# The weighted values of a unit in two halves, with scores and a tile of row maxima between

## The chip, the core and the metric

The kernel runs on one core of a Trainium2 chip. Its engines are TensorE (matmuls; in the profile PE, its weight loads PEld), VectorE (DVE), ScalarE (ACT), GpSimd (POOL) and SyncE (SP, which issues most DMAs). They run side by side, each in its own program order, and wait for each other by semaphores. The metric is the device time of one execution in microseconds.

## The reference

Input are 64 sequences x of 128 tokens with 128 features, a side input of the same shape, and a context of 64 x 120 x 128. Layer one is

```
x = x + L0_xattn(layernorm(x), side, ctx, ctx)   # 16 heads of 8, 128 + 120 keys
x = x + L0_ffn(layernorm(x))                     # top 2 of 8 experts, 352 wide
```

and layer two has the same form: attention over the 120 context keys, then a gelu layer with the top 2 of 8 experts. In the attention of layer one, queries come from the normalised x, the first 128 keys and values from the side input by projection, the other 120 keys and values are the context itself. Scores are q.k / sqrt(8), softmax over all 248 keys, weighted values, an output projection with bias, and the residual.

## The kernel before

The 64 sequences are handled in 16 groups of four. Layer one's attention runs first, with the routing of its expert layer beside it; then come the expert matmuls (135 tiles of 128 routed rows), then layer two's attention and its expert layer. The change touches layer one's attention alone.

One step of the loop handles one group g and has 8 units: unit u is one sequence (u // 2) and one half of its 16 heads (u % 2). What a unit issues, and in which order, is a list written by hand, UNIT (line 144). Every engine walks through the same list and takes what concerns it:

- "scores" i, four a unit (line 979, matmuls in line 993): transposed scores of four heads, keys in the partitions, for group g. Places 0 and 2 have the 128 side keys, 1 and 3 the 120 context keys. Four matmuls of 128 columns, into one of three PSUM tiles (ps_sc). The row maxima are already in the contraction as rows of their own. ScalarE takes each tile through the exponent into p (line 674).
- "max" i, four a unit (matmuls in line 1006): scores of the *next* group g+1, two heads a tile, queries in the partitions, 2 matmuls of 248 columns into one of two PSUM tiles (ps_mx). VectorE reduces each to its negated row maxima (row_maxima, line 822). Behind the reduction stand small pieces of statistics and routing (between, INPUT_STAGES, ROUTE_STAGES).
- "values" 0 and 1 (weighted_values, matmuls in line 1030): the weighted values of the unit *before*, of one half of its eight heads each. 18 columns of weights (8 value columns and one of ones for each of two heads), four strips of 32 output partitions, float32: 8 matmuls a half, which the trace records as 16. Half 0 waits for the exponents of places 0 and 1 of the unit before, half 1 for those of 2 and 3, and signals pv_done when it is through. The same PSUM tile ps_o collects four units; after units 0 and 4 ScalarE evicts it to o_sb (line 703) once pv_done has reached the unit, and behind its exponents of that unit.
- "job" 0, 1 and 2: what the list jobs (line 127) puts at this place of this unit: transposes (XT, line 939; AT of the attention's output, line 963; OB of the values, line 959; MT of the maxima, line 955; RX), projections (QP, KP, VP, OP), router matmuls (RQ line 1349, RC). They share two PSUM tiles (misc) in turn, so a job waits until the one before the last has been evicted.

TensorE takes all four kinds, ScalarE "scores" and "job", VectorE "max" and "job". pv_done is also what ScalarE waits for before it writes the first exponent of a unit into p's tile of two units before.

Of the kernel before, what the change touches and what calls it, by code (L numbers as in the profile page):

```python
# [101 lines left out]
def attention_layer(nc, x_in, x_out, side_t_in, ctx_in, ctx_t_in, layer, consts, route, stacks, second, expert_w=None,  # L102
# [40 lines left out]
    if first:  # L143
        UNIT = [
            ("job", 0), ("scores", 0), ("max", 0), ("scores", 1), ("job", 1), ("max", 1), ("values", 0),
            ("values", 1), ("scores", 2), ("max", 2), ("scores", 3), ("job", 2), ("max", 3),]
    else:
        UNIT = [
            ("job", 0), ("scores", 0), ("max", 0), ("scores", 1), ("values", 0), ("values", 1), ("job", 1),
            ("max", 1),]  # L150
# [1855 lines left out]
def encoder(nc, a, out):  # L2006

    x3 = nc.dram_tensor("x3", (NG, S, GB, D), F32, kind="Internal").ap()
    xs = nc.dram_tensor("routed_in", (ROUTED_ROWS, ROW), F32, kind="Internal").ap()
    ys = nc.dram_tensor("routed_out", (TOKENS * TOP + 2 * E * S, D), F32, kind="Internal").ap()  # L2010
    x1, second = (ys[0:TOKENS * TOP].rearrange("(g k s b) d -> k g s b d", k=TOP, s=S, b=GB)[k] for k in range(TOP))
    with ExitStack() as c:
        route, stacks = Route(nc, c, xs), Stacks(nc, c)
        consts = constants(nc, c, a["w_attn"], a["b_attn"], a["b_rows"], a["wqkv_t"], route)
        attention_layer(nc, a["x"], x1, a["side_t"], a["ctx"], a["ctx_t"], 0, consts[0], route, stacks, second,
                        expert_w=(a["w1_t"], a["w2_t"]))
        expert_tiles(nc, ys, route, stacks)
        head = AdapterHead(nc, c, route, x3, a["wg_t"], a["bg"], a["W1_t"], a["W2_t"])
        attention_layer(nc, x1, x3, None, None, a["ctx_t"], 1, consts[1], route, stacks, second, head=head)
        adapter_layer(nc, x3, out, head)  # L2020
# [46 lines left out]
```

## Time and profile before

| | |
|---|---|
| median of 3 runs | 1438.31 us (1438.08 to 1440.24) |
| profiled execution | 1436.72 us |
| its span, first to last instruction | 1434.9 us |
| mean granted TensorE clock | 0.956 of full speed |
| weighted values in layer one | first block 73.9 us, last 577 us into the span |

The span is what the trace covers; the profiled execution's own time has 1.8 us around it. The page's busy times are by engine over the whole span. For the change one reads the stretch of layer one: how long a group takes there, and at which times TensorE starts each block of matmuls. Starts are measured; ends of matmuls are modelled, so a block's cost is read from its start to the start of the next.

### The profile page before, as it was taken

The page shows a single profiled execution, that of the slowest core. Times are in us where ns is not written, and L with a number is a line of the kernel's source. Part 1 is how long each engine was busy: PE and PEld are TensorE (multiplying, and loading weights), DVE is VectorE, ACT ScalarE, POOL GpSimd, SP SyncE. Part 2 cuts the span into 40 slices and gives each one's busy share as a digit, 9 for nine tenths or more (in the row PEclk, how much of TensorE's full clock was granted, in tenths as well). Part 3 has the DMA queues.
Part 4 walks back from the last instruction along what each step waited for, and adds up shares of the span by engine and source line. Part 5 has one row for each costly group of instructions (what it writes and reads, how often), then busy time and mean ns, then how long its engine had stood idle before and what let it go on. Part 6 is the DMA issues. An engine that isn't in the chain of part 4 may idle for free. (4 is left out here: it accounts for less than half of the span.)

```text
span 1434.9 us, 44416 instructions
## 1 busy us (share of the span) xinstructions
PE 1271.0 (89%) x16309; PEld 1052.2 (73%) x16309; DVE 1083.2 (75%) x3396; ACT 828.7 (58%) x1582; POOL 875.1 (61%) x947
## 2 busy tenths in 40 slices
PE   1789999999999999279999999669999999869997
PEld 0367787777777787279999999437777778746775
DVE  6778999989988896547766666458888888736663
ACT  1167777767777767156666666235666666534452
POOL 5346888888888856547777777544555544136650
PEclk9799999999999999689999999879999999979999
DMA  5676677777777760535555554588888887445765
GB/s 167 220 220 212 216 248 245 235 225 251 240 233 225 219 193 30 194 53 64 65 65 65 64 65 63 103 235 224 265 271 268 260 264 234 127 104 120 178 166 131
DMA packets 212422, 252.15 MB, mean 176 GB/s; under 512 B 38256, under 2 KB 173680, under 8 KB 205040
## 3 DMA queue, kind: packets, MB, share of 16 engines
q1 hardware_dynamic: 179552, 226.33, 52.7%
q0 software_dynamic: 25840, 21.71, 10.8%
q8 instruction: 131, 2.15, 0.6%
q10 hardware_dynamic: 6816, 1.29, 0.5%
q14 instruction: 83, 0.68, 0.1%
HBM read 156.73 MB, written 91.46 MB: 173 GB/s over the span
## 5 line engine op out<-in xcount | busy, mean ns | idle before, releaser
L822 DVE TENSOR_REDUCE L_neg_max<-L_ps_mx 128x2 f32<-128x496 f32 (+1 forms) x768 | 489.1, 660 | 93.4 <-PE L_ps_mx L1006 90.7
L674 ACT ACTIVATE L_p<-L_ps_sc 120x512 f32<-120x512 f32 (+1 forms) x768 | 417.3, 598 | 207.5 <-PE L_ps_sc L993 203.9
L1006 PE MATMUL L_ps_mx<-stack_k,stack_q 118*128 118x248 bf16 (+1 forms) x2048 | 299.7, 251 | 45.8 <-DMA stack_q<-L_q_rows 29.9
L993 PE MATMUL L_ps_sc<-stack_q,stack_k 122*120 122x128 bf16 (+1 forms) x3072 | 300.3, 222 | 5.0 <-DMA stack_q<-L_mT 2.4
L993 PEld LDWEIGHTS L_ps_sc<-stack_q,stack_k 122*120 122x120 bf16 (+1 forms) x3072 | 239.3, 123 | 58.2 <-issue 34.4
L1507 POOL DMA_INDIRECT routed_out<-M_y,M_x x135 | 211.9, 1570 | 88.5 <-DVE M_y L1598 87.3
L1030 PE MATMUL L_ps_o<-L_p,L_v 120*18 120x128 f32 (+1 forms) x6144 | 219.7, 275 | 3.3 <-ACT L_o_sb L703 2.9
L1006 PEld LDWEIGHTS L_ps_mx<-stack_k,stack_q 118*128 118x128 bf16 x2048 | 141.9, 100 | 106.7 <-issue 36.5
L1030 PEld LDWEIGHTS L_ps_o<-L_p,L_v 120*18 120x18 f32 (+1 forms) x6144 | 147.3, 98 | 38.1 <-issue 24.8
L1377 POOL DMA_INDIRECT routed_in<-R_xn,R_slot x128 | 127.1, 993 | 42.5 <-issue 35.9
L1553 ACT COPY M_w<-stack_k 128x768 f32 x135 | 112.1, 832 | 53.9 <-PE M_ps_g L1530 36.9
L1530 PE MATMUL M_ps_a<-M_xT,M_w 128*128 128x128 f32 x810 | 114.0, 278 | 0.0
L1530 PE MATMUL M_ps_g<-M_xT,M_w 128*128 128x128 f32 x810 | 113.4, 277 | 0.0
L1539 PE MATMUL M_ps_y<-M_w,M_hT 128*128 128x128 f32 x810 | 112.7, 276 | 0.0
L488 POOL TENSOR_TENSOR L_rem<-L_qf,L_q_parts_sb 128x512 f32<-128x512 f32 x30 | 34.8, 1161 | 121.4 <-ACT L_q_parts_sb L619 121.4
L1558 ACT ACTIVATE M_act_a<-M_ps_a 128x384 f32<-128x384 f32 x135 | 66.2, 491 | 73.4 <-PE M_ps_a L1530 72.4
L1530 PEld LDWEIGHTS M_ps_a<-M_xT,M_w 128*128 128x128 f32 x810 | 102.4, 194 | 0.1
L1530 PEld LDWEIGHTS M_ps_g<-M_xT,M_w 128*128 128x128 f32 x810 | 102.3, 194 | 0.0
L1539 PEld LDWEIGHTS M_ps_y<-M_w,M_hT 128*128 128x128 f32 x810 | 101.3, 192 | 0.2 <-DVE M_hT L1590 0.2
L1579 DVE COPY M_w<-stack_q 128x384 f32 x135 | 49.1, 363 | 63.7 <-issue 61.5
L1590 DVE TENSOR_TENSOR M_hT<-M_act_a,M_ps_g 128x384 f32<-128x384 f32 x135 | 74.8, 554 | 27.5 <-ACT M_act_a L1558 22.8
L1967 DVE TENSOR_TENSOR F_hg<-F_h,F_spread 128x512 f32<-128x512 f32 x64 | 41.3, 689 | 48.5 <-DMA F_spread<-F_gate_rows 39.5
(210 smaller groups left out, 2127.3 us busy)
## 6 DMA issues: line engine op xcount, KB each, us to landing
L_q_rows<-L_q_parts_sb SPq DMA_DIRECT2D x192, 192.0 KB, 4.1
stack_q<-L_q_rows SPq DMA_DIRECT2D x192, 192.0 KB
stack_k<-L_k_rows SPq DMA_DIRECT2D x96, 372.0 KB
stack_k<-L_k_rows SPq DMA_DIRECT2D x96, 180.0 KB
F_spread<-F_gate_rows SPq DMA_DIRECT2D x32, 512.0 KB, 6.5
L_k_rows<-L_k_parts_sb SPq DMA_DIRECT2D x32, 372.0 KB, 4.2
M_x<-routed_in SPq DMA_DIRECT2D x135, 66.0 KB, 2.0
L_k_rows<-L_k_parts_sb SPq DMA_DIRECT2D x32, 180.0 KB, 4.2
```

What stands on the lines that cost most here:

```text
L674: nc.scalar.activation(p_t[t][u % 2][:, quarter * 4 * S:(quarter + 1) * 4 * S], ps_sc[n % NSC][0:KEYS[t], :], ACT.Exp).then_inc(sc_read, 1)
L822: nc.vector.tensor_reduce(neg_max[:, b, kk * HPB:(kk + 1) * HPB], v, AX.X, ALU.max, negate=True).then_inc(max_read, 1)
L993: last = mm(ps_sc[n % NSC][0:KEYS[t], j * S:(j + 1) * S], k_st[p][:, b // 2, h, b % 2, k0:k0 + KEYS[t]], q_st[p][:, b // 2, h, b % 2], sta ...
L1006: last = mm(ps_mx[i % NMX][:, j * NK:(j + 1) * NK], q_st[p][0:TERM_TOP, b // 2, h, b % 2], k_st[p][0:TERM_TOP, b // 2, h, b % 2], start=Tr ...
L1030: last = mm(ps_o[r:r + 2 * (DH + 1), col:col + S], v_t[t][p][:, b, at:at + 2 * (DH + 1)], p_t[t][u % 2][:, j * S:(j + 1) * S], start=(t == ...
L1377: self.nc.gpsimd.indirect_dma_start(out=self.route.xs, out_offset=bass.IndirectOffsetOnAxis(ap=self.slot[g.par][:, b, k:k + 1], axis=0), i ...
L1507: nc.gpsimd.indirect_dma_start(out=ys, out_offset=bass.IndirectOffsetOnAxis(ap=token_row, axis=0), in_=y_t[ts % NY][:], in_offset=None, co ...
L1530: last = nc.tensor.matmul(out[:, k * S:(k + 1) * S], w1[th % NW][:, half + k * 128:half + (k + 1) * 128], xT[p][:], start=True, stop=True)
L1539: last = nc.tensor.matmul(ps_y[p][:, 0:D], hT[p][:, k * S:(k + 1) * S], w2[ty % NW][:, k * D:(k + 1) * D], start=(k == 0), stop=(k == FC - 1))
L1553: nc.scalar.copy(w1[tw % NW][:], w1_all[:, bass.ds(e_w * W1, W1)]).then_inc(w1_ready, 1)
L1558: nc.scalar.activation(act_a[p][:], ps_a[p][:, 0:FC * S], ACT.Silu).then_inc(silu_ready, 1)
L1590: nc.vector.tensor_tensor(hT[p][:], act_a[p][:], ps_g[p][:, 0:FC * S], ALU.mult).then_inc(hT_ready, 1)
```

## The change

In layer one's UNIT the entry ("values", 1) moves from directly behind ("values", 0) to behind ("max", 2), ahead of ("scores", 3). By count of places the tiles of row maxima are max 0 to 3, so it stands between the third and the fourth. Nothing else is edited, and layer two's list is unchanged.

```
     if first:
         UNIT = [
             ("job", 0), ("scores", 0), ("max", 0), ("scores", 1), ("job", 1), ("max", 1), ("values", 0),
-            ("values", 1), ("scores", 2), ("max", 2), ("scores", 3), ("job", 2), ("max", 3),]
+            ("scores", 2), ("max", 2), ("values", 1), ("scores", 3), ("job", 2), ("max", 3),]
```

## Rows read from the trace of the kernel before

**Rows 1.** The page, busy time by engine over the span.

```profile
PE 1271.0 (89%) x16309; PEld 1052.2 (73%) x16309; DVE 1083.2 (75%) x3396; ACT 828.7 (58%) x1582; POOL 875.1 (61%) x947
```

**Rows 2.** Windows of one group: length; busy PE, PEld, DVE, ACT, POOL; clock; DMA.

```profile
169.64:201.62 31.98, 31.32 (x514) 25.43 (x513) 29.56 (x98) 23.39 (x49) 27.54 (x31) 1.00 0.77 241
331.55:363.54 31.99, 31.32 (x514) 25.43 (x513) 29.57 (x98) 23.39 (x49) 27.55 (x31) 1.00 0.74 235
```

**Rows 3.** Waits in 331.55 to 363.54: us in total, times, longest.

```profile
DVE L_neg_max L822 <- PE L_ps_mx L1006: 1.9, 4, 0.9
```

**Rows 4.** Timeline of TensorE, 387.9 to 389.7: start, length, instructions.

```profile
387.92 0.38 PE L1006 MATMUL L_ps_mx<-stack_k,stack_q 118*128 118x248 bf16 x2
388.23 1.08 PE L1030 MATMUL L_ps_o<-L_p,L_v 128*18 128x128 f32 x32
389.24 0.40 PE L993 MATMUL L_ps_sc<-stack_q,stack_k 122*128 122x128 bf16 x4
389.47 0.38 PE L1006 MATMUL L_ps_mx<-stack_k,stack_q 118*128 118x248 bf16 x2
389.69 0.39 PE L993 MATMUL L_ps_sc<-stack_q,stack_k 122*120 122x128 bf16 x4
```

**Rows 5.** Timeline, unit 5: start and last four of one block of values.

```profile
348.96 0.53 PE L1030 MATMUL L_ps_o<-L_p,L_v 128*18 128x128 f32 x12
...
349.74 0.29 PE L1030 MATMUL L_ps_o<-L_p,L_v 120*18 120x128 f32 x4
349.97 0.40 PE L993 MATMUL L_ps_sc<-stack_q,stack_k 122*128 122x128 bf16 x4
```

**Rows 6.** Timeline, units 4 and 5: TensorE, and ScalarE's chain beside it.

```profile
346.50 0.39 PE L993 MATMUL L_ps_sc<-stack_q,stack_k 122*120 122x128 bf16 x4
346.98 0.39 PE L1006 MATMUL L_ps_mx<-stack_k,stack_q 118*128 118x248 bf16 x2
347.29 0.24 PE L955 MATMUL L_misc<-C_ident_bf,L_m_parts 128*64 128x128 bf16 x1
347.47 0.40 PE L993 MATMUL L_ps_sc<-stack_q,stack_k 122*128 122x128 bf16 x4
...
347.92 0.27 ACT L634 COPY L_mT<-L_misc 64x128 bf16<-64x128 bf16 x1
...
348.19 0.63 PE L959 MATMUL L_misc<-C_ident,L_o_sb 128*128 128x128 f32 x4
```

**Rows 7.** Timeline, start of unit 6: TensorE's scores and maxima, VectorE's reductions.

```profile
350.65 1.83 DVE L822 TENSOR_REDUCE L_neg_max<-L_ps_mx 128x2 f32<-128x496 f32 x3
...
350.86 0.39 PE L993 MATMUL L_ps_sc<-stack_q,stack_k 122*128 122x128 bf16 x4
351.37 0.39 PE L1006 MATMUL L_ps_mx<-stack_k,stack_q 118*128 118x248 bf16 x2
```

**Rows 8.** Timeline, end of unit 7 and start of unit 0.

```profile
357.49 0.38 PE L1006 MATMUL L_ps_mx<-stack_k,stack_q 118*128 118x248 bf16 x2
...
357.90 1.26 DVE L822 TENSOR_REDUCE L_neg_max<-L_ps_mx 128x2 f32<-128x496 f32 x2 [0.24 <-PE L_ps_mx L1006]
...
358.14 0.39 PE L993 MATMUL L_ps_sc<-stack_q,stack_k 122*128 122x128 bf16 x4
358.73 0.37 PE L1006 MATMUL L_ps_mx<-stack_k,stack_q 118*128 118x248 bf16 x2 [0.20 <-DVE L_neg_max L822]
...
359.22 0.39 PE L1006 MATMUL L_ps_mx<-stack_k,stack_q 118*128 118x248 bf16 x2
```

**Rows 9.** Timeline, units 0 and 2: VectorE's pair of reductions, and TensorE's job AT.

```profile
361.22 1.36 DVE L822 TENSOR_REDUCE L_neg_max<-L_ps_mx 128x2 f32<-128x496 f32 x2
...
366.75 0.39 PE L993 MATMUL L_ps_sc<-stack_q,stack_k 122*120 122x128 bf16 x4
367.39 0.63 PE L963 MATMUL L_misc<-C_ident,L_att 128*128 128x128 f32 x4 [0.25 <-DVE L_att L757]
```

**Rows 10.** Timeline, unit 1 of an earlier group: the key projection.

```profile
297.66 1.10 PE L946 MATMUL L_misc<-L_srcT,C_w 128*128 128x512 f32 x2 [1.51 <-DMA L_srcT<-in_side_t]
```

More of the change, by code:

```diff
@@ L145, in attention_layer @@
             ("job", 0), ("scores", 0), ("max", 0), ("scores", 1), ("job", 1), ("max", 1), ("values", 0),
-            ("values", 1), ("scores", 2), ("max", 2), ("scores", 3), ("job", 2), ("max", 3),]
+            ("scores", 2), ("max", 2), ("values", 1), ("scores", 3), ("job", 2), ("max", 3),]
     else:
```

## The prediction

> **What bounds the kernel now.** I read the page's busy shares, then the busy time of single groups of layer one, then the waits in one of them, then TensorE's order of time unit by unit. The page gives TensorE 89% of the span and no other engine over 75% [rows 1], but that is a mean over stages. In layer one the work repeats every 31.98 or 31.99 us, with 514 recorded matmuls each time: TensorE is busy 31.3 of the 32.0 us, VectorE 29.6, ScalarE 23.4, at a granted clock of 1.00, which is the 2.4 GHz level [rows 2]. The reader should doubt the 31.3, since matmul ends are modelled, and look at starts instead: inside a unit each block starts when the one before it has streamed: four scores take 0.22 to 0.23 us, a tile of maxima 0.22, and only a few waits stand between. VectorE itself waits four times for a tile, 1.9 us [rows 3]. So TensorE is the bound most of the time; VectorE takes over in stretches. The waits that I find between TensorE's starts, each what a step took over its usual 0.22 us, are 0.26 us in unit 4, 0.29 from unit 5 to 6, 0.36 and 0.05 from unit 7 to 0, and 0.41 ahead of the transposes of the attention in unit 2: about 1.4 us of 32 [rows 6 to 9].
>
> **The price of a switch.** The weighted values are matmuls with 18 columns of weights, written to four strips, and everything around them uses 120 or 128 columns. A tile of maxima is followed by scores after 0.22 us, but by values after 0.31: 0.09 to go in [rows 4]. Within a block of values four strips start every 0.11 us (28 matmuls in 349.74 - 348.96 = 0.78). The last four are followed by scores after 0.23 instead of 0.11: 0.12 to come out [rows 5]. The 64-column transpose of the maxima pays the same: 0.31 into it, and 0.18 out of it where a 128-column matmul at full rate leaves after 0.05 [rows 6]. There is no wait in this that another engine could end sooner: it stands in every unit, also where all inputs are old. I call it a switch: in and out cost 0.09 + 0.12 = 0.21 us.
>
> **The change, part by part.** Only TensorE's order changes, since VectorE and ScalarE skip the "values" entries and keep theirs; no DMA, no job and no matmul is added or removed. (1) The 32 matmul records of a unit's values were one block of 1.01 us; they become two of 16 with scores and a tile of maxima between. That is one switch more in each of 16 x 8 = 128 units: 0.21 x 128 = 26.9 us if nothing hides it. (2) The third scores and the third tile of maxima come 0.44 us earlier behind the first half: counted from the start of the first half, third scores at 0.56 (was 1.01), third maxima 0.80 (1.24), second half 1.10, fourth scores 1.67 (1.46), fourth maxima 1.90 (1.68). VectorE gets its third tile 0.44 us earlier and its fourth 0.22 later; ScalarE likewise. (3) The count that releases the probability tile comes 0.66 us or so later: with switch, half a block and the scores and maxima between. Queued behind it is only the first exponent of the next unit, whose scores come at least 0.8 us behind the second half, and the eviction of the values, which stands behind the fourth exponent anyway. I take nothing for it; if that cover failed, it would cost at most the 0.66 us in the two units a group that evict, 1.3 us a group, less than nothing I exclude, as no producer gets faster by it.
>
> **What of the 0.21 lies beside a wait.** I follow one group, lateness against the old times:
> - Units 2 to 3, 3 to 4 and 6 to 7 have no TensorE wait: +0.21 each, +0.64.
> - Unit 4: the fourth maxima waited 0.26 us for VectorE (346.50 to 346.98 instead of 0.22) [rows 6], so they start when they did, but the fourth scores are 0.21 later, and from them hangs ScalarE's chain of exponent, eviction of the values, copy of the maxima (347.92), whose bank the transposes of the values take at 348.19. The old exponent had started 0.05 behind its scores' readiness, so this chain is 0.16 later: +0.16.
> - Unit 5 to 6: 0.51 instead of 0.22 between scores and maxima, as VectorE runs three reductions without a gap [rows 7]. The lateness that TensorE brings is swallowed but for what VectorE's own chain has been set back: -0.07.
> - Unit 7 to 0: no job stands between. The first maxima of unit 0 waited for the reduction that began at 357.90 [rows 8]; that tile comes earlier now, and this 0.36 goes. What is late next is the second one: it needs the fourth maxima of unit 7 read, which lie ready 0.41 us behind the start of their matmuls (357.49 to 357.90), at 1.68 + 0.41 before and at 1.90 + 0.41 now; plus 0.68 for the reduction and 0.06 from its end to the next tile (357.90 + 1.26 to 359.22) [rows 8] it is 3.05 against 2.78 by TensorE. 3.05 + 0.31 = 3.36 to the next values, was 3.28: +0.07.
> - Units 0 to 2: the 0.41 before the transposes at 367.39 [rows 9] is VectorE's backlog. It would hide 0.43 almost whole, but the backlog itself moves: in unit 0 the pair of reductions takes 1.36 us instead of 1.25 [rows 9], so it already waits for the fourth tile, which is now 0.21 later. +0.22.
> Sum: 0.64 + 0.16 - 0.07 + 0.07 + 0.22 = 1.02 us a group, 0.7 of 1.7 hidden. Over 16 groups 16.3 us. Bounds from the same rows: all 1.4 us of waits hidden leaves 1.7 - 1.4 = 0.3 a group, 5 us; none hidden 26.9. The first group has more waits, and three groups wait for the side input (at 297.66 for 1.51 us in the row [rows 10]), which more time per group can only shorten: I take 1.0 off, an estimate with ends of 0 and 4. The sum is +15.3 us.
>
> The profiled execution took 1436.7 us, span 1434.9; it becomes 1452.0. The median of the runs is 1438.3, 1.6 above, and becomes **1453.6 us**. What comes behind layer one starts when its last group is done, so I shift it whole.
>
> **A rule to weigh.** By starts TensorE sets the pace, and by busy time VectorE has 29.6 of 32.0 us [rows 2]. The Trainium skill (Perfetto Trace Analysis, Identifying the Most-Contended Engine) says that TensorE's matmul busy share misleads and is to be judged by its weight loads' share; by that TensorE has 25.4 of 32.0, VectorE is the busiest, and the switches would be free. That is rival C below; I trust the starts over the shares.
>
> **Rivals.**
> - A, nothing hidden: +26.9 us, 1465. For it: three units of eight have no wait at all, and new waits could replace those removed. Against: the waits in units 4, 5 and 2 are set by VectorE, whose work is unchanged.
> - B, nearly all hidden: +5 us, 1443. For it: waits of 1.4 us a group and VectorE at 92%. Against: waits hide only what comes ahead of them in the same stretch, and VectorE has gaps of 0.2 to 0.9 us in units 6 to 7 that show TensorE as the bound there.
> - C, VectorE is the bound and the extra lies beside it: within 0.2%, 1438. Against: VectorE waits 1.9 us a group for tiles [rows 3].
> - D, the other side: faster. One mechanism: a 16-record block enters and leaves without the drain, since its neighbours are ready, and the earlier third tile takes away the waits at 358.73 and in unit 5. Without a price the third tile 0.44 earlier saves 0.14 us in unit 7 to 0 and up to 0.29 in unit 5 to 6: 0.43 a group, 7 us, 1431. It decides from a switch of under 0.7 / 8 = 0.09 us, the part that waits can hide. Against: the 64-column transpose, a block of a single matmul, pays full price in and out.
>
> **Chances.** Forecast 0.70 (+9 to +21 us), A 0.12, B 0.09, C 0.04, D 0.05. A measurement can tell about 0.2%, 3 us. The range 1443 to 1465 leaves out C, D and part of A. Faster 0.05, same 0.04, slower 0.91.
>
> **What would show it.** In the changed kernel: two values blocks of some 0.56 us from start to following scores, each entered 0.31 behind a tile of maxima or, for the second, likewise; a unit without waits 0.21 longer; steady groups of about 33.0 us; VectorE's waits for tiles grown to some 2.9 us a group; no wait at the first maxima of unit 0, one of 0.27 at the second; the wait before the attention's transposes down to 0.2 or less. Stages behind layer one keep their length. Wrong it would be if a half block left in under 0.5 us, or if the groups stayed at 32.0 us.

## The result, and the profile after

The changed kernel takes 1456.79 us in the median of four runs, the kernel before 1439.28 beside it: a ratio of 1.0124 with an interval of 1.0083 to 1.0164, slower, +17.5 us. Run again in five rounds, it gave 1454.26 us against the 1439.53 of before, +14.7 us, and a ratio of 1.0097 (1.0062 to 1.0132). The forecast was 1453.6, range 1443 to 1465. The profiled execution took 1463.31 us, span 1461.5, which is the slowest of the four; so it has to be read by stages before anything is concluded from it.

The windows of the four stages, before: layer one's attention, its routing end and experts, layer two's attention, the rest. Columns: stretch, its length, then busy PE, PEld, DVE, ACT, POOL with counts, granted clock, DMA share, GB/s.

```profile
73.90:577.40 503.50, 483.44 (x8009) 391.70 (x8008) 441.88 (x1407) 361.33 (x738) 386.74 (x437) 1.00 0.69 213
577.40:970.50 393.10, 330.99 (x2825) 316.29 (x2813) 251.02 (x756) 200.80 (x310) 253.54 (x179) 0.91 0.52 95
970.50:1267.40 296.90, 278.46 (x4523) 223.09 (x4522) 249.04 (x719) 186.07 (x366) 131.34 (x150) 0.99 0.77 230
1267.40:1434.90 167.50, 145.56 (x850) 106.82 (x838) 90.59 (x414) 67.05 (x146) 72.11 (x136) 0.93 0.61 148
```

The same stages of the changed kernel.

```profile
73.90:595.30 521.40, 513.65 (x8005) 373.55 (x8008) 449.14 (x1407) 371.49 (x739) 385.46 (x437) 1.00 0.66 205
595.30:991.20 395.90, 331.62 (x2825) 316.65 (x2815) 251.26 (x756) 200.95 (x310) 253.68 (x179) 0.90 0.53 95
991.20:1293.10 301.90, 281.26 (x4524) 225.01 (x4522) 248.49 (x719) 186.62 (x366) 131.33 (x150) 0.97 0.76 226
1293.10:1461.50 168.40, 147.04 (x846) 108.86 (x838) 90.27 (x414) 67.36 (x146) 70.86 (x136) 0.91 0.62 147
```

And of the changed kernel in its second profile.

```profile
74.30:596.90 522.60, 513.99 (x8009) 373.68 (x8008) 449.16 (x1407) 371.57 (x739) 385.46 (x437) 1.00 0.66 205
596.90:989.60 392.70, 331.52 (x2825) 316.90 (x2813) 251.03 (x756) 200.82 (x310) 253.75 (x179) 0.90 0.52 96
989.60:1284.00 294.40, 278.44 (x4523) 224.00 (x4522) 248.06 (x719) 185.40 (x366) 131.43 (x150) 0.98 0.77 232
1284.00:1448.60 164.60, 143.11 (x850) 105.35 (x838) 90.36 (x414) 67.30 (x146) 72.07 (x136) 0.94 0.64 151
```

Layer one's attention is 17.9 and 19.1 us longer than before. The other three stages together were 8.7 us longer in the first profile and 5.8 us shorter in the second, with the same code, so that difference does not repeat, and only the first row is put down to the change. TensorE's weight loads even became less busy in it (391.7 to 373.6), though nothing of its work went.

A steady group of the changed kernel, the answer to [rows 2]: the same 514 matmuls in 33.67 instead of 31.98 us.

```profile
339.17:372.84 33.67, 33.40 (x514) 24.25 (x513) 30.17 (x97) 24.14 (x49) 27.38 (x32) 1.00 0.72 227
```

TensorE's order of time in unit 2, which has no wait in it, answers to [rows 4].

```profile
312.00 0.63 PE L1030 MATMUL L_ps_o<-L_p,L_v 128*18 128x128 f32 x16
312.57 0.40 PE L993 MATMUL L_ps_sc<-stack_q,stack_k 122*128 122x128 bf16 x4
312.80 0.38 PE L1006 MATMUL L_ps_mx<-stack_k,stack_q 118*128 118x248 bf16 x2
313.11 0.64 PE L1030 MATMUL L_ps_o<-L_p,L_v 128*18 128x128 f32 x16
313.67 0.43 PE L993 MATMUL L_ps_sc<-stack_q,stack_k 122*120 122x128 bf16 x4
313.94 1.08 PE L942 MATMUL L_misc<-L_xnT,C_w 128*128 128x512 f32 x2
```

Each half block takes 0.56 to 0.57 us to the scores behind it, the second is entered 0.31 behind its tile of maxima, as the prediction laid out. But the scores behind the second half take 0.27 (313.67 to 313.94), where the same scores took 0.22 before. The end of unit 7 and unit 0, TensorE, answers to [rows 8].

```profile
335.27 0.39 PE L993 MATMUL L_ps_sc<-stack_q,stack_k 122*128 122x128 bf16 x4
335.49 0.38 PE L1006 MATMUL L_ps_mx<-stack_k,stack_q 118*128 118x248 bf16 x2
335.70 0.39 PE L993 MATMUL L_ps_sc<-stack_q,stack_k 122*120 122x128 bf16 x4
336.20 0.39 PE L1006 MATMUL L_ps_mx<-stack_k,stack_q 118*128 118x248 bf16 x2
...
337.08 0.40 PE L993 MATMUL L_ps_sc<-stack_q,stack_k 122*128 122x128 bf16 x4
337.53 0.39 PE L1006 MATMUL L_ps_mx<-stack_k,stack_q 118*128 118x248 bf16 x2
```

The first maxima of unit 0 (335.49) no longer wait; the second (336.20) wait 0.27, both as foreseen. The third (337.53) wait 0.22: this was not. VectorE shows why.

```profile
336.06 0.41 DVE L1220 TENSOR_TENSOR R_products<-R_products,R_max 128x256 f32<-128x256 f32 x1
...
336.80 1.25 DVE L822 TENSOR_REDUCE L_neg_max<-L_ps_mx 128x2 f32<-128x496 f32 x2
...
339.37 0.68 DVE L822 TENSOR_REDUCE L_neg_max<-L_ps_mx 128x2 f32<-128x496 f32 x1 [0.41 <-PE L_ps_mx L1006]
```

The first reduction of unit 0 begins at 336.80 behind a routing step and the split of the maxima, and the third tile needs its PSUM buffer. Later VectorE idles 0.41 us for the fourth tile. In the waits of a group, VectorE's for tiles of maxima went from 1.9 us in four [rows 3] to

```profile
DVE L_neg_max L822 <- PE L_ps_mx L1006: 2.8, 7, 0.8
```

### The profile page after: what moved, and what is told of

It is laid out like the page before. It is cut to its first block and busy times, and to the rows that moved or that the text cites. A ratio compares the mean times of both kernels' runs of the same rounds, so it can differ in the third digit from the quotient of the medians.

```text
span 1461.5 us, 44416 instructions
## 1 busy us (share of the span) xinstructions
PE 1307.3 (89%) x16309; PEld 1038.9 (71%) x16309; DVE 1090.5 (75%) x3396; ACT 839.7 (57%) x1582; POOL 872.7 (60%) x947
## 5 line engine op out<-in xcount | busy, mean ns | idle before, releaser
L674 ACT ACTIVATE L_p<-L_ps_sc 120x512 f32<-120x512 f32 (+1 forms) x768 | 427.7, 598 | 218.9 <-PE L_ps_sc L993 215.3
L993 PE MATMUL L_ps_sc<-stack_q,stack_k 122*120 122x128 bf16 (+1 forms) x3072 | 307.4, 224 | 5.5 <-DMA stack_q<-L_mT 2.9
L993 PEld LDWEIGHTS L_ps_sc<-stack_q,stack_k 122*120 122x120 bf16 (+1 forms) x3072 | 233.7, 123 | 83.9 <-ACT L_p L674 39.4
L1030 PE MATMUL L_ps_o<-L_p,L_v 120*18 120x128 f32 (+1 forms) x6144 | 245.2, 277 | 2.4 <-ACT L_o_sb L703 2.3
L1030 PEld LDWEIGHTS L_ps_o<-L_p,L_v 120*18 120x18 f32 (+1 forms) x6144 | 136.6, 98 | 63.0 <-issue 42.4
L488 POOL TENSOR_TENSOR L_rem<-L_kf,L_k_parts_sb 128x512 f32<-128x512 f32 (+1 forms) x23 | 27.7, 1206 | 94.2 <-ACT L_k_parts_sb L624 67.7
```

Source lines behind the costliest of these rows:

```text
L674: nc.scalar.activation(p_t[t][u % 2][:, quarter * 4 * S:(quarter + 1) * 4 * S], ps_sc[n % NSC][0:KEYS[t], :], ACT.Exp).then_inc(sc_read, 1)
L993: last = mm(ps_sc[n % NSC][0:KEYS[t], j * S:(j + 1) * S], k_st[p][:, b // 2, h, b % 2, k0:k0 + KEYS[t]], q_st[p][:, b // 2, h, b % 2], sta ...
L1030: last = mm(ps_o[r:r + 2 * (DH + 1), col:col + S], v_t[t][p][:, b, at:at + 2 * (DH + 1)], p_t[t][u % 2][:, j * S:(j + 1) * S], start=(t == ...
```

## The experiments

Group lengths below are from the start of one key projection to the next, in the steady part of layer one; in most runs the steady groups agree to 0.02 us. Each variant was profiled once (the changed kernel twice), so its group lengths come from one execution. Totals are against 17 to 35 runs of the kernel before, whose times spread from 1429 to 1454 us, so below 0.3% the group tells more than the total.

**The changed kernel again** (after2).

> The changed kernel again, in five rounds against the kernel before. Layer one's steady groups 33.7 us as in its first profile (32.0 before), layer one's attention +17 to +18 us. What lies behind layer one (8.7 us longer in the first profile) should not repeat, if it is chance in the clock and the DMAs of layer two: total +15 to +20 us; if it belongs to the change, +25 us.

Layer one as at first, steady groups 33.66 to 33.68 us (two late ones 33.81 and 33.74), attention +19.1; total +14.7 us. The stages behind did not repeat their loss, as shown above.

**One block, moved as a whole** (block_late).

```
-("values", 0), ("values", 1), ("scores", 2), ("max", 2), ("scores", 3), ...
+("scores", 2), ("max", 2), ("values", 0), ("values", 1), ("scores", 3), ...
```

> Both halves of the values behind the third tile of maxima, so one block of values a unit as in the kernel before, but the third scores and maxima stand ahead of it. If the loss comes from the extra switch in and out of the 18-column matmuls (0.21 us a unit), it is gone here: steady groups of 32.0 to 32.4 us, total within 8 us of before. The upper end holds if the 0.05 us more that the 120-column scores took behind values in the changed kernel (0.27 instead of 0.22) is a price of what follows a block: 8 x 0.05 = 0.4 us a group, 5 to 6 us. Rival: the loss comes from the order (third tile early, fourth late, VectorE's backlog in unit 0): then the fourth tile, later still here, costs as much as in the changed kernel or more, groups of 33.7 us or longer, +18 us.

The switch theory's number was wrong here, and the rival's came true: ratio 1.0146 (1.0111 to 1.0181), groups of 34.03 us, without any extra switch. TensorE, units 2 and 3:

```profile
349.55 1.08 PE L1030 MATMUL L_ps_o<-L_p,L_v 128*18 128x128 f32 x32
350.55 0.43 PE L993 MATMUL L_ps_sc<-stack_q,stack_k 122*120 122x128 bf16 x4
350.82 1.08 PE L942 MATMUL L_misc<-L_xnT,C_w 128*128 128x512 f32 x2
...
353.73 0.39 PE L993 MATMUL L_ps_sc<-stack_q,stack_k 122*128 122x128 bf16 x4
354.40 0.39 PE L1006 MATMUL L_ps_mx<-stack_k,stack_q 118*128 118x248 bf16 x2 [0.29 <-DVE L_neg_max L822]
```

Two things are seen. The block costs its old 1.00 us and the scores behind it 0.27: so the 0.05 us belongs to 120-column scores right behind values, not to the split. And three tiles of maxima now stand ahead of the values, for two buffers, so the third waits for VectorE (0.67 us instead of 0.22 from 353.73). Order alone can cost as much as the switches do; this run does not say which of the two the changed kernel pays.

**Only the third scores between the halves** (split_s2).

```
-("values", 0), ("values", 1), ("scores", 2), ("max", 2), ...
+("values", 0), ("scores", 2), ("values", 1), ("max", 2), ...
```

> Split as in the changed kernel, but only the third scores stand between the halves, and the second half is followed by a tile of maxima with 128-column weights. Switch theory: one more switch a unit at 0.21 us, without the 0.05 us of the 120-column scores; units that have no wait 0.20 to 0.22 us longer than before (2 to 3: 4.68 becomes 4.89), third tile of maxima only 0.2 us later than in the kernel before, so no new wait at unit 0's third tile. Groups of 33.0 to 33.5 us, +13 to +18 us in all. Order theory: the third and fourth tile come nearly when they did before, so nearly nothing is lost, under +4 us.

Ratio 1.0101 (1.0065 to 1.0138), groups of 33.52 us, at the upper edge of the switch theory's 33.0 to 33.5 and far from the order theory. Here the order is nearly that of before.

```profile
284.08 0.63 PE L1030 MATMUL L_ps_o<-L_p,L_v 128*18 128x128 f32 x16
284.65 0.40 PE L993 MATMUL L_ps_sc<-stack_q,stack_k 122*128 122x128 bf16 x4
284.98 0.63 PE L1030 MATMUL L_ps_o<-L_p,L_v 128*18 128x128 f32 x16
285.55 0.39 PE L1006 MATMUL L_ps_mx<-stack_k,stack_q 118*128 118x248 bf16 x2
285.77 0.39 PE L993 MATMUL L_ps_sc<-stack_q,stack_k 122*120 122x128 bf16 x4
```

From the first half to the fourth scores it is 1.69 us, before 1.46: 0.23 a unit, and the fourth scores behind a tile of maxima take 0.22 again.

**A small matmul between the halves, 128 or 18 columns wide** (dummy_wide, dummy_narrow). Nothing is moved; the small matmul goes into a tile that the third scores overwrite.

```
 elif what == "values" and gp.exists:
+    if first and i == 1 and g.exists:
+        n = sc_no(g, u, 2)
+        wait(pe, sc_read, n - NSC + 1)
+        mm(ps_sc[n % NSC][0:W, 0:8], ident_bf[:, 0:W], ident_bf[:, 0:8], ...)   # W = 128 or 18
     weighted_values(gp, up, i)
```

> The order of the kernel before, with one small matmul more between the two halves of every unit's values in layer one: 128 columns of weights, 8 columns streamed, into a score tile that the third scores overwrite. The order of all real work stays, so only the switch out of the 18-column matmuls and back in is added. Switch theory: between the last four matmuls of the first half and the first four of the second 0.11 + 0.21 = 0.32 us or a little more (the small matmul itself 0.03), units without waits 0.24 us longer; some of it is hidden in the waits of units 1, 4, 5 and 7, groups of 33.0 to 33.5 us (31.98 before). Order theory: the loss in the changed kernel comes from the moved tiles; nothing is moved here, so groups of 32.0 to 32.3 us.

> The control of the run with the small matmul between the halves: the same small matmul, but with 18 columns of weights into 18 partitions, like its neighbours. Switch theory: no change of the array's form, so 0.11 to 0.15 us between the halves' fours instead of 0.32, units at most 0.03 to 0.05 us longer, groups of 32.0 to 32.3 us. If what costs is any break in the run of equal matmuls, it is as slow as with 128 columns.

The wide one:

```profile
207.04 0.63 PE L1030 MATMUL L_ps_o<-L_p,L_v 128*18 128x128 f32 x16
207.61 0.18 PE L1052 MATMUL L_ps_sc<-C_ident_bf 128*128 128x8 bf16 x1
...
208.28 0.40 PE L993 MATMUL L_ps_sc<-stack_q,stack_k 122*128 122x128 bf16 x4
```

The narrow one:

```profile
400.60 0.64 PE L1030 MATMUL L_ps_o<-L_p,L_v 128*18 128x128 f32 x16
401.05 0.17 PE L1052 MATMUL L_ps_sc<-C_ident_bf 128*18 128x8 bf16 x1
...
401.61 0.40 PE L993 MATMUL L_ps_sc<-stack_q,stack_k 122*128 122x128 bf16 x4
```

From the first half to the scores it is 1.24 us with 128 columns, 1.01 with 18, and 1.01 in the kernel before [rows 4]. The same instruction at the same place costs 0.23 us or nothing, by its width alone. It is not the type either: both small matmuls are bf16 between float32 ones, and the narrow one is free. Groups 33.62 and 32.02 us; ratios 1.0122 (1.0086 to 1.0158) and 0.9993 (0.9962 to 1.0024). This settles the price of a switch (the 0.23 us includes the small matmul itself), and that the new order is not needed to lose 1.6 us a group. The 33.62 lies above the 33.0 to 33.5 that I had written: less is hidden in waits than I thought. The Trainium skill (TensorEngine Tiling (Array Packing), Tiling Modes) says that changing the tiling mode drains the TensorE; the trace agrees in so far as each change of width costs time, in and out together 0.21 to 0.23 us here; that the time is a drain, no run shows.

**The new order in two units only** (split_15, split_26) and **in all but unit 0** (split_not0). TensorE's walk takes the changed list for the units named, otherwise the old one.

```
-for what, i in UNIT:
+for what, i in SPLIT_UNIT if first and u in (1, 5) else UNIT:   # or (2, 6), or (1, 2, ..., 7)
```

> The changed order in units 1 and 5 only, the old one in the other six. These two run into waits of their own for VectorE in the kernel before (0.41 us ahead of the attention's transposes, 0.29 us ahead of unit 6's first maxima). By my account the extra 0.26 us of each is hidden there: groups of 32.0 to 32.1 us, total within 1 us. If hiding doesn't work so (VectorE's own chain starts later by as much), 0.5 us a group: 32.5 us.

> The changed order in units 2 and 6 only, the counterpart of the run with units 1 and 5. In the kernel before these two have no wait behind them that VectorE set beforehand: VectorE itself waits for TensorE's tiles there. The extra 0.26 us of each stays: groups of 32.4 to 32.5 us (31.98 before). If a wait anywhere in the group could hide a switch anywhere, it would be 32.0 us as with units 1 and 5.

> The changed order in units 1 to 7, the old one in unit 0. In the changed kernel unit 0's third tile of maxima waits 0.22 us for VectorE's backlog, and its fourth comes late for VectorE, which sets the wait ahead of the attention's transposes. With the old order there, unit 0 is 0.48 us shorter, but the transposes' wait grows from 0.15 us by what VectorE doesn't gain: VectorE's tile comes some 0.3 us earlier, so groups of 33.3 to 33.45 us (33.67 with all eight). If unit 0's new waits cost nothing beyond the switch, only 0.26 us or less is gained: 33.4 to 33.5; if nothing behind unit 0 hung on it, 33.2.

One window of a group in each, first units 1 and 5,

```profile
231.03:263.01 31.98, 31.70 (x514) 25.14 (x513) 29.66 (x98) 23.43 (x49) 27.54 (x32) 1.00 0.76 238
```

then units 2 and 6,

```profile
464.06:496.64 32.58, 31.90 (x513) 25.20 (x513) 28.83 (x96) 22.60 (x47) 26.71 (x31) 1.00 0.71 224
```

then all but unit 0.

```profile
203.29:236.40 33.11, 32.91 (x514) 24.40 (x513) 30.08 (x98) 23.95 (x49) 27.41 (x32) 1.00 0.73 229
```

Two switches in units 1 and 5 cost nothing (most steady groups 31.98 to 32.06 us); two in units 2 and 6 cost 0.53 (steady groups from 32.51), their full 2 x 0.26. Whether a switch costs depends on whether the wait behind it was set before the switch. Leaving unit 0 out gives back 0.56 of the 1.69 us (33.11 us), more than the 0.2 to 0.35 that I expected, and the wait ahead of the attention's transposes stays at 0.15 us instead of growing: VectorE's chain is then early by all of TensorE's gain, so it had been TensorE, by unit 0's tiles, that held it back. Totals: 1.0030 (1.0000 to 1.0060), 1.0009 (0.9974 to 1.0044), 1.0069 (1.0034 to 1.0103). The first two can't be told apart by total time.

**The side input loaded earlier** (src_early).

```
 load_k(0)
 ...
+if first and g3.exists:
+    load_src(g3)
 load_q(0)
 ...
-if first:
-    if g3.exists:
-        load_src(g3)
```

> The kernel before with the load of the side input issued ahead of the loads and writes of the queries instead of behind them. In the profile of before three groups waited for it, 4.2 us in all, in the changed kernel none. If the loads are late because they stand behind the bulk transfers in the queue, the waits at the key projection go: -2 to -4 us, groups all at 32.0 us. If they are late by a disturbance of the DMA engines in that run alone, no difference beyond 1 us.

I had expected 2 to 4 us less; it is slower, 1.0042 (1.0016 to 1.0068). TensorE's waits from 110 to 560 us in the kernel before, three of six lines:

```profile
PE L_misc L963 <- DVE L_att L757: 4.0, 14, 0.6
PE L_misc L946 <- DMA L_srcT<-in_side_t: 3.6, 3, 1.5
PE L_ps_mx L1006 <- DMA stack_q<-L_q_rows: 1.1, 2, 0.6
```

and with the early load, the first line of three:

```profile
PE L_ps_mx L1007 <- DMA stack_q<-L_q_rows: 8.9, 9, 2.2
```

The wait for the side input is gone, and the one for the queries, whose load now stands behind it, has grown from 1.1 to 8.9 us. So the early load moved the wait to the next transfer and did not remove it. In the changed kernel the same list has one line, and it holds neither DMA:

```profile
PE L_misc L963 <- DVE L_att L757: 0.2, 1, 0.2
```

Behind the third group, the kernels with groups of up to 32.6 us (before, src_early, dummy_narrow, split_15, split_26, mt_wide, at_late, at_late_mt_wide) each have one to five groups more than 0.5 us over their steady length; those with 33.1 us or more (changed, twice, split_s2, block_late, split_not0) have none, and dummy_wide one.

**A way to something faster** (mt_wide, at_late, at_late_mt_wide).

```
-m_parts = ... [S, 2, H, 2]      +m_parts = ... [S, 4, H, 2]   # rest zero
-transpose(misc[0:4 * H, ...     +transpose(misc[:, ...        # mt_wide
-(2, 1, "AT", 0)                 +(2, 2, "AT", 0)              # at_late
```

> The kernel before, with the transposes of the row maxima (4 a group in both layers' 32 steps, two in a step) made 128 columns wide: the tile of maxima parts gets 64 zero columns more, whose result nobody reads. In the profile of before such a transpose takes 0.31 us to enter and 0.18 to leave, against 0.22 and 0.05 to 0.06 for 128-column neighbours. If the price hangs on the width of the weights, both fall and each saves 0.2 us: two a group in layer one, 0.4 us, groups of 31.6 us, where no wait of VectorE takes it; total -4 to -8 us, and faster than both kernels. If the price comes from the transpose or its wait, nothing changes.

> The kernel before with the transposes of the attention (job AT) one place later in unit 2, ahead of the query projection instead of ahead of the second maxima. TensorE waits there 0.41 us a group for VectorE. One place later VectorE is through, so the wait goes: groups of 31.6 to 31.7 us, -4 to -6 us. If VectorE is the bound of this stretch and TensorE would only wait elsewhere (for the tiles of unit 2 or 3), 32.0 us as before.

> The later AT and the 128-column transposes of the maxima together. The latter alone took 0.14 us a group. Groups of 31.4 to 31.6 us, 5 to 9 us less than before, if both hold; this is the version that may beat both kernels. If the two gains take the same slack, it is no better than the later AT alone.

The wide transpose, unit 0 of the first of these (the same transposes as the one of unit 5 in [rows 6]):

```profile
360.26 0.39 PE L995 MATMUL L_ps_sc<-stack_q,stack_k 122*120 122x128 bf16 x4
360.49 0.22 PE L957 MATMUL L_misc<-C_ident_bf,L_m_parts 128*128 128x128 bf16 x1
360.55 0.38 PE L1008 MATMUL L_ps_mx<-stack_k,stack_q 118*128 118x248 bf16 x2
```

It is entered after 0.23 and left after 0.06, where unit 0 of the kernel before has 0.32 and 0.18: the price hangs on the width of the weights. But the steady group fell only from 31.98 to 31.84 us. The other transpose's gain, in unit 5, turned into waits behind it: from the maxima ahead of it to the transposes of the values it is 1.22 us (before 1.21). The total is 0.9988 (0.9966 to 1.0010), no change that can be told. The later AT removed its wait of 0.41 us and put a longer one, 0.91 us (1.13 between the starts, usually 0.22), before the tile of maxima ahead of the values:

```profile
336.35 0.39 PE L993 MATMUL L_ps_sc<-stack_q,stack_k 122*120 122x128 bf16 x4
337.48 0.39 PE L1006 MATMUL L_ps_mx<-stack_k,stack_q 118*128 118x248 bf16 x2 [0.74 <-DVE L_neg_max L822]
```

Groups 32.37 us, 1.0034 (0.9999 to 1.0069); with the wide transposes 32.18 us, 0.9992 (0.9966 to 1.0018). VectorE's backlog was the bound there, as the second theory had it, and the group grew by 0.4 us where that theory had it unchanged. No version here beats the kernel before measurably.

## Why the prediction was right, and which terms were not

**The direction and its cause** were right, and are shown: one more switch a unit, 0.21 us by the rows of before, 0.23 in split_s2 and dummy_wide, nothing in dummy_narrow. Rival D, a switch that costs nothing, falls with it, and C too: with VectorE as the bound the time would have stayed, but it went up while both VectorE's share and the weight loads' share of a group fell (29.6 of 32.0 to 30.2 of 33.7, and 25.4 to 24.3 us).

**The group came out at +1.69 us, not +1.02.** By pieces from values to values, forecast and measured:

| from unit to unit | forecast | measured (before to after) |
|---|---|---|
| 2 to 3, 3 to 4, 6 to 7 | +0.21 each | +0.26 each (4.68 to 4.94, 4.16 to 4.42, 3.68 to 3.94) |
| 4 to 5 | +0.16 | +0.21 (3.92 to 4.13) |
| 5 to 6 | -0.07 | +0.07 (3.61 to 3.68) |
| 7 to 0 | +0.07 | +0.12 (3.28 to 3.40) |
| 0 to 2 | +0.22 | +0.50 (4.01 to 4.50, then 4.66 in both) |

Three terms failed. The first is the price in part (1): I took the exit from one kind of follower, 128-column scores, and the second half is followed by 120-column ones. That is 0.05 us more, 0.4 a group, and block_late shows it without a split. The second is the step "the backlog itself moves" in units 0 to 2: I followed the fourth tile and not the third, which now comes before its buffer is free (0.22 us). The wait ahead of AT hid unit 1's switch whole (4.66 us in both kernels from unit 1 to 2) and nothing of unit 0's; split_not0 shows that unit 0 brings 0.56 of the 1.69. The third and smallest is the -0.07 from unit 5 to 6: beyond the 0.05 of the price, 0.09 us less was hidden there. What I said of the waits held: the fourth maxima of unit 4 and the first of unit 0 don't wait any more, the second maxima of unit 0 wait 0.27, AT waits 0.15; the eviction chain in unit 5 is late by 0.21 where I had 0.16. Part (3), taken at nothing, held too: from 110 to 560 us the list of waits has none of ScalarE for the weighted values.

What the new order does beside the switch is seen against dummy_wide, which has the switch and the old order (medians of the groups between 200 and 480 us). From unit 5 to 6 and 7 to 0 it takes 3.82 and 3.52 us, the changed kernel 3.68 and 3.40: there the earlier third tile probably hides part of the switch. From unit 0 to 1 it takes 4.24 and the changed kernel 4.50. The order gives and takes nearly the same, and the groups end 0.05 us apart (33.62 and 33.67).

**That the total fell so near the forecast was luck.** A steady group lost 1.69 us, which is rival A's 1.68 (0.21 x 8, nothing hidden) and not my 1.02: the dearer price and unit 0's new wait made up for what was hidden. With +1.02 a group I had 16.3, minus 1.0 for the first group and late side inputs. From the third to the last of the 16 key projections, 13 groups, 422.0 us became 436.9: +14.8 instead of 13 x 1.69 = 22.0. (What lies behind the last one adds 3.0, which gives the stage's +17.9.) Of the 7.2 us between, 4.8 are the three groups of 33.9, 33.3 and 33.6 us that waited for DMAs before (3.6 and 1.1 us in the list above) and don't now, and 1.8 is the first of the 13, which takes 33.6 us in both kernels. I had bounded this term at 0 to 4 and taken 1, so it fell outside its own bounds. Two errors, 0.67 x 13 = 8.7 us too little for the groups and 7.2 - 1.0 = 6.2 too little for what they hide of waits that were there before, nearly cancelled. That longer groups make the DMA waits go fits the list of kernels above; but it is a count over single profiles, not a run made for it, and why a transfer is late in one group and not in another stays open.

**Shifting all behind layer one whole** held on the mean of two profiles (+8.7 and -5.8 us), no better.

## What to carry to other kernels

Before moving a narrow block of matmuls, count how often the array's form changes in the program's order, and price one change by the starts on both sides and by what will follow it; keep narrow blocks whole. A switch or any extra work is free only ahead of a wait that was already set by another engine, and costs its full time elsewhere, so go unit by unit, and follow each moved tile to its buffer as well as to its reader. A small total with large cancelling parts is only found by looking at the steady group and at the odd groups apart.

## What the runs showed of the hardware

A matmul with 18 columns of weights in a run of such matmuls costs 0.005 us (dummy_narrow), one with 128 columns and as many columns streamed costs 0.23 (dummy_wide). The weight loads of 120-column scores take 133 ns on the mean, those of 128 columns 98, in the kernel before:

```profile
L993 PEld LDWEIGHTS L_ps_sc<-stack_q,stack_k 122*120 122x120 bf16 x820 | 71.2, 133 | 3.0 <-ACT L_p L674 0.8
...
L993 PEld LDWEIGHTS L_ps_sc<-stack_q,stack_k 122*128 122x128 bf16 x820 | 52.6, 98 | 29.0 <-issue 22.5 <-ACT L_p L674 4.8
```

Between other wide matmuls that difference is hidden, 0.22 us for either; right behind narrow ones 120-column scores take 0.27 (the changed kernel, block_late) and 128-column scores 0.23. That the slower weight load is the cause is likely and not shown. The Trainium skill (TensorE: Matmul & The Clock Gate, Weight-path perf modes) says that the fast weight load is on when the number of weights is 128 and the type is not FP32; the two rows fit it, but no run made the scores 128 columns wide to test it.
